# Gated expert mixture: GpSimd waits for one tile's scattered rows to land before it sends the next tile's

## What is computed

```python
x = x + 0.5 * _L0_ffn_ref(_layernorm(x), ...)   # gated mixture, first call
x = x + _L0_attn_ref(_layernorm(x), ...)        # attention with a memory
x = x + 0.5 * _L0_ffn_ref(_layernorm(x), ...)   # gated mixture, second call
x = x + 0.5 * _L1_ffn_ref(_layernorm(x), ...)   # silu mixture, first call
x = x + _L1_attn_ref(_layernorm(x), ...)        # attention in a band
x = x + 0.5 * _L1_ffn_ref(_layernorm(x), ...)   # silu mixture, second call
```

## Time and profile before

| what | value |
|---|---|
| time, median of 3 runs | 2465.71 us (2459.22 to 2470.34) |
| span of the profiled execution | 2596.9 us |
| PE, DVE, ACT, POOL busy in the span | 78%, 68%, 54%, 44% |
| indirect transfers of the gated tile phases (L451) | 156, busy 152.5 us |
| indirect transfers of the silu tile phases (L451) | 156, busy 178.0 us |

### The profile page before, as it was taken

One profiled execution on the slowest core, in us unless ns is written; L12 is line 12 of the kernel. 1 busy time (PEld: TensorE's weight loads), 2 busy tenths in 40 slices (PEclk: granted clock), 3 DMA queues, 4 the chain that ended last, 5 costly groups with the idle time before them and its releaser, 6 DMA issues. The chain is left out here.

```text
span 2596.9 us, 85429 instructions
## 1 busy us (share of the span) xinstructions
PE 2013.5 (78%) x34490; PEld 1682.7 (65%) x34490; DVE 1771.5 (68%) x4346; ACT 1399.1 (54%) x2304; POOL 1150.4 (44%) x1073
## 2 busy tenths in 40 slices
PE   3767569999999998577738899564666689768895
PEld 2557468888888887456726799452222278647895
DVE  4666578888888888666755444676999965454443
ACT  1546534444455554345725455257999956545452
POOL 3645545666656665463535466355000000045463
PEclk8778889999999999578868999786555556669997
DMA  5122310000000000012241222202333220021324
GB/s 123 39 77 72 92 58 1 0 0 0 0 0 0 0 0 2 22 58 76 73 149 49 73 76 63 76 1 35 63 53 61 49 65 8 3 91 42 86 78 122
DMA packets 112885, 125.53 MB, mean 48 GB/s; under 512 B 24248, under 2 KB 94504, under 8 KB 112064
## 3 DMA queue, kind: packets, MB, share of 16 engines
q1 hardware_dynamic: 91760, 84.85, 13.5%
q0 software_dynamic: 18176, 37.79, 4.4%
q10 hardware_dynamic: 2768, 0.55, 0.2%
HBM read 60.00 MB, written 46.20 MB: 41 GB/s over the span
## 5 line engine op out<-in xcount | busy, mean ns | idle before, releaser
L2623 DVE CUSTOM_DVE_ANT_0 be_logs<-be_joint,be_logs 128x1024 f32<-128x1024 f32 x256 | 293.3, 1220 | 10.2 <-ACT be_logs L2606 9.1
L2606 ACT ACTIVATE be_logs<-be_joint,b_tiny 128x1024 f32<-128x1024 f32 x256 | 283.8, 1114 | 19.6 <-PE be_joint L2591 11.8
L2591 PE MATMUL be_joint<-be_parts_k,be_parts_q 64*128 64x512 f32 x512 | 202.3, 789 | 108.8 <-DVE be_sums L2623 91.4
L451 POOL DMA_INDIRECT d_pairs<-s_y_tile,s_x_tiles x156 | 178.0, 1141 | 128.1 <-DVE s_y_tile L1426 101.8
L2591 PEld LDWEIGHTS be_joint<-be_parts_k,be_parts_q 64*128 64x128 f32 x512 | 73.7, 285 | 237.3 <-DVE be_sums L2623 216.5
L451 POOL DMA_INDIRECT d_pairs<-g_y_tile,g_x_tiles x156 | 152.5, 978 | 166.6 <-ACT g_y_tile L901 122.5
L1260 PE MATMUL s_ps_y<-s_down,s_a_tile 128*128 x1248 | 151.8, 275 | 0.0
L1426 DVE TENSOR_SCALAR s_y_tile<-s_ps_y,s_x_tiles 128x128 f32<-128x128 f32 x156 | 47.6, 347 | 147.8 <-PE s_ps_y L1260 100.8
L1260 PEld LDWEIGHTS s_ps_y<-s_down,s_a_tile 128*128 128x128 f32 x1248 | 145.9, 192 | 0.0
L1540 PE MATMUL m_front<-m_xnT,m_w_rot 128*128 128x128 f32 x1024 | 143.4, 284 | 3.2 <-DVE m_turned_q L1857 3.2
L1336 ACT ACTIVATE s_a_tile<-s_ps_h,s_tile_bias 128x256 f32<-128x256 f32 x312 | 122.3, 475 | 32.8 <-PE s_ps_h L1243 32.6
(11 more groups left out here) (504 smaller groups left out, 6271.2 us busy)
## 6 DMA issues: line engine op xcount, KB each, us to landing
g_x_tiles<-d_rows SPq DMA_DIRECT2D x78, 132.0 KB
s_x_tiles<-d_rows SPq DMA_DIRECT2D x78, 132.0 KB
bw_v<-b_v SPq DMA_DIRECT2D x64, 68.0 KB, 2.1
d_rows<-d_rows SPq DMA_DIRECT2D x32, 132.0 KB
s_down<-L_ffn_We SPq DMA_DIRECT2D x16, 256.0 KB, 5.4
be_parts_q<-be_high_q SPq DMA_DIRECT2D x64, 64.0 KB, 2.3
be_parts_q<-b_soft_q SPq DMA_DIRECT2D x64, 64.0 KB, 2.3
be_parts_k<-be_high_k SPq DMA_DIRECT2D x60, 64.0 KB, 2.3
```

The lines of the kernel that those rows point to most:

```text
L451: nc.gpsimd.indirect_dma_start(out=pairs[:, :], out_offset=bass.IndirectOffsetOnAxis(ap=x_tile[i % LOADS_AHEAD][:, h, D:D + 1].bitcast(U32 ...
L2591: last = nc.tensor.matmul(joint_ps[k % DEPTH][:, a, :], parts[b % 2][0][rows, i * P:(i + 1) * P], parts[b % 2][1][rows, half * 512:(half + ...
L2606: nc.scalar.activation(logs[k % DEPTH][:, :, :], joint_ps[k % DEPTH][:, :, :], ACT.Ln, bias=A.tiny[:, :]).then_inc(s.log_ready, 1)
L2623: nc.vector.tensor_tensor_reduce(out=flat, in0=joint_ps[k % DEPTH][:, :, :].rearrange("p a j -> p (a j)"), in1=flat, scale=1.0, scalar=0.0 ...
```

## The change

Before GpSimd handles tile i of the second phase, from the second tile on, it waits until both transfers of tile i-1 have landed. The wait stands in the loop of `gated_stage`, so it holds for both gated calls and not for the silu stages. Nothing else is changed; the number of transfers, their sizes and their queue are the same.

```diff
             for i in range(MAX_TILES):
+                if i:
+                    pool.wait_ge(s.y_sent[(i - 1) % Y_TILES], 32 * ((i - 1) // Y_TILES + 1))
                 dispatch.pool_tile_back(pool, i, K.pairs, x_tile, y_tile)
```

## The result

The kernel with the change takes 2572.66 us (median of 4 runs, 2563.69 to 2578.52) against 2468.03 us for the kernel before (4 runs): a ratio of 1.042, 95% interval 1.0388 to 1.0453, or 104.6 us. It is slower, inside the predicted range of 2480 to 2592, and 24 us above the predicted 2549.

A forecast was written before the change was run, and what follows sets the result against it. PE was taken to pace gated tiles at 2.70 us without stalls. With the wait a step is 1.26 + 2.33 + 0.20 = 3.79 us, costing 83 us: 2465.7 + 83 = 2549 us, range 2480 to 2592.

The forecast's parts named there:

- The predicted 3.79 us: Gated tile step with the wait: 1.26 to second transfer, 2.33 to landing, 0.20 restart; ends 3.59 and 4.34 us.
- the two bases: Cost in gated phases against the profiled execution, 21 us, or against timed runs assumed without most stalls, 83 us (chosen).
- Rival (a): Gated phases: unexplained stalls are in the timed runs too; cost 21 us, 2487 us; chance 0.14.
- (b): Gated phases: stalls in timed runs, GpSimd starts at once on landing; step 3.59, cost 6 us, 2472 us; chance 0.08.
- (e): Gated phases faster: stalls go with the bursts, free restart, landings under 2.1 us; 11 us gained, 2454 us; chance 0.03.
- Without them PE sets the pace: Gated phases before the change, without stalls: PE at granted clock 0.88 takes 2.70 us a tile.
- one row of 4.10: SP's next load once started 4.10 us after a second transfer, not 2.33; left to the range.
- The span should grow by some 20 us: Sign in the profile after: span up some 20 us only, timed median up four times that.
- The restart: GpSimd's delay from landing to next tile's first transfer: 0.20 us taken, between nothing and 0.75 us.
- Its row of 0.75 us: Upper end for GpSimd's restart: from the end of ACT's y half to the transfer's start, in the kernel before.
- rival (c): Gated phases: GpSimd's restart takes the full 0.75 us; step 4.34, cost 125 us, 2590 us; chance 0.12.
- Rival (d): Gated phases: PE loses its clock, needs 4.05 us a tile and becomes the bound; 103 us, 2568 us; chance 0.05.

The follow-up runs named there:

- the kernel's second trace: The kernel before the change, unedited, profiled once more; it took 2459.55 us in this execution.
- the silu kernel: The change's wait moved to the same loop of `silu_stage`, gated stage as in the kernel before; 2512.0 us, ratio 1.0166.

## Why the prediction was right, and where its sizes were off

**What the wait does** was right in each part. The step is one chain, issue, landing, restart; GpSimd waits for its own landing in 37 of 38 steps by the rows, and in the 38th too by the trace; the second transfers still follow at 1.26 us; a landing two tiles back costs nothing. The predicted 3.79 us is 3.76 to 3.77 measured, by the same terms: 1.26, then 2.38 to SP's start where 2.33 was taken, then 0.12 for GpSimd where 0.20 was taken. That these two small errors cancel is luck.

**The choice between the two bases** was right as well. Rival (a) falls with the kernel's second trace: no such stalls, 2.54 us a tile. So does (b), for the same reason: its cost of 6 us stood on a step of 3.5 that the timed runs don't have. (e) needed the same stalls, and landings under 2.1 us; transfers that went alone stood 2.50 us apart.

**The step before was mis-sized.** "Without them PE sets the pace" and its 2.70 us don't hold: the granted clock of 0.88 in the earlier trace rows came from the execution with the stalls. Undisturbed it is 0.96, PE is done sooner, and GpSimd's own 2.52 us of the earlier trace rows is the pace (2.54 measured). That is 76 x 0.16 = 12 us too little cost.

**Late landings were left to the range.** The prediction took every landing at 2.33 us; it had one row of 4.10 and left it out of the sum. The means are 3.99 and 3.87 us against 3.76, so they cost 38 x (0.23 + 0.11) = 13 us. With both, and the step 0.03 shorter: 83 + 12 + 13 - 2 = 106 us, against 104.6.

**"The span should grow by some 20 us" was wrong**: it fell by 35. The sum took the stalls as hidden behind GpSimd, but had just put them down to the one execution; then they could not be expected in the next trace either, nor the rest of its 131 us, which lies outside these phases. Only the other half of the sentence, the growth of the timed median, was a test.

**The restart** came out near the predicted end, but for a condition that the prediction didn't see. It reasoned that 0.45 us of a wait is done ahead while GpSimd stands idle. That is so where the landing's wait is written first and stands on the transfer itself. Its row of 0.75 us was of the other kind: in the kernel before, the wait for ACT's half stands on the instruction ahead, which ran at 186.18, and the transfer started at 186.90. Where the landing is waited for in that way, the 0.46 us stay on the path, with steps of 4.2 to 4.3 us, and rival (c) would have been the nearer forecast, at 2613 to 2621 us measured. The Trainium skill ("Perfetto Trace Analysis", section "DMA Instruction — SWDGE (GPSIMD)") says that a transfer is put into a wait queue and the sequencer goes on to decode; the Trainium skill ("Perfetto Trace Analysis", section "Identifying Dependency Chains") says that further waits may be put in as instructions of their own ahead of it. No run here shows the first by itself. The traces agree with the second, and show which waits those are: all but the one written first, with 0.27 us from the landing to the start of a transfer that carries its wait, and 0.73 to 0.78 where such an instruction carries it.

**Rival (d)** doesn't decide. The granted clock did fall, from 0.96 to 0.84 and 0.88, but PE is busy for 99.5 of 155 us and waits for ACT.

By the Trainium skill's figure for one transfer ("DMA: Bandwidth & Descriptors", section "Anatomy of one DMA — SWDGE (gpsimd) path") the prediction had a step of 3.61 us as an estimate; 3.76 is measured, and the measurement decides.

## What to carry to other kernels

Before a wait on a completed transfer goes into a loop, add up issue, start to landing and restart, and hold the sum against the step of an undisturbed execution: the price is the difference for each step, and one more tile in flight made it nothing here. When a profile's span lies well above the timed runs, take a second trace before using its paces; a clock or a step from such a trace is as suspect as its stalls. Where an instruction waits for several things, write the wait for the one that comes last first, and test the order: it was worth 32 to 42 us here, and the rows of the slower orders put the wait down to ACT or to issue, not to the landing.

## What the runs showed of the hardware that was not expected

- *The order of three waits on one transfer is worth 0.46 us a time*: 2.50 us from a transfer to the next one that its landing releases with that wait first, 2.97 and 3.00 in second and third place, 3.08 with the wait on an instruction of its own. The wait written first stands on the transfer itself, the other two on an instruction ahead of it. The transfer starts 0.27 us after a landing that releases it, and 0.70 us after the end of that instruction where the landing releases the instruction.
- *GpSimd issues one 128-row indirect transfer every 1.26 us* (0.96 busy and 0.30 between) where nothing holds it; at two a tile this alone bounds the gated phases at 2.52 us a tile.
- *A landing is late about every sixth tile.* Most landings take 2.24 us from the transfer's start. In the changed kernel the steps that end at 193.66 and 217.01 are 23.35 us apart; six steps are five of 3.76 and one of 4.5. With two landings a tile a long wait ends at 203.56 and the next at 238.18, 34.6 us apart, or again six tiles of some 5.46, one of them longer. So they go with the work done and not with time. Around the first of them, and not in the 7 us before, the list of DMA queues of the changed kernel (packets, MB, share of 16 engines) has a packet of a queue that carries instructions:

```profile
q8 instruction: 1, 0.02, 1.3%
```

  The trace holds more than this one. In the two phases of the changed kernel ten landings take over 2.8 us; in nine of them such a packet of 16384 bytes is under way between the transfer's start and its landing, and the tenth is the step of 7.50 us with the attention loads. Three more packets of these phases delay no landing. The 5.67 us step of the silu kernel has such a packet too (at 1388.05). That these packets delay the landings is argued from the time they come at, and was not tested. The Trainium skill ("Runtime: NRT & Kernel Launch", section "Instruction fetch mechanics") says that an engine's instructions are fetched in blocks of 16 KiB; the 16384 bytes of the packet agree with that.
